# Four column groups for the time-kernel products, eight kernel writes on another queue, and a later second Toeplitz piece

## The chip, the core and the metric

One core of one Trainium2 chip runs the whole program. The metric is the device time of one execution in microseconds (us), and the median over several executions counts.

## What is computed

The input x has 32 rows of 32 channels by 512 steps, that is 1024 tokens of 512 numbers. Two layers follow each other. What matters here, cut from the reference:

```python
# layer 0: a condition matrix per row, then a routed feed-forward net
xt = einsum('bct,bcd->bdt', x, W[condition])          # 1024 tokens of 512
gate = top 2 of 16 experts per token
y  = sum over experts of gate * (silu(xt@w1+b1) * (xt@w2+b2)) @ w3 + b3
z  = silu(xt@sw1+sb1) * (xt@sw2+sb2) @ sw3 + sb3      # shared part
x  = x + y + z
# layer 1: a state space convolution over time, 32 heads, 512 steps
dtA = (-exp(log_A_real) + 1j*A_imag) * exp(log_dt)[:, None]
Cs = C * (exp(dtA) - 1) / A
K  = 2 * einsum('hn,hnl->hl', Cs, exp(dtA * arange(512))).real   # kernel: 32 heads x 512
y  = causal convolution of x (masked by length) with K, plus x * D
x  = x + feed-forward net and layer norm of y
```

The change is about K: how it is computed, written to memory, and read back as a Toeplitz matrix.

## The kernel before

**The expert blocks.** The (token, expert) pairs are sorted into 31 blocks of 128 rows (NB = 31, loop variable n, lines 1512 to 1544 on TensorE). For block n TensorE does 16 matmul instructions for w1 and w2 (L1518), the product with w3 of block n-2 (`block_y`, L1491), and four transposes of the rows of block n+2 (`transpose_x`, L1485). ScalarE makes silu (`bsil`, L771) of block n and copies the transposed rows of block n+2 (`xt`, L759). VectorE makes `bhid` (L1151) and copies block n-2's result into `yout` (L1143), which raises `yout_ok`. GpSimd gathers the token rows of a block from memory (`xg`, L597) and scatters each finished block to `ytok` (L604), seven blocks behind the gathers, by the function `move`.

**The weights.** `ew` is a ring of 14 slots for expert weights (w1 and w2 at 256 KB each by L501, w3 at 256 KB by L503). The queue of SyncE (SP) issues the loads. It runs a loop over n: wait for `yout_ok` n+1, then the loads that `load_step` puts at this n (the loads of blocks 14 to 27 at steps 0 to 18, the last of these at step 18; the loads of blocks 28, 29 and 30 at steps 22, 23 and 24), then possibly a Toeplitz piece.

**The time kernel.** K of a head at time 32 i + j is a product of powers: one factor for i (`lre_k`, `lim_k`: 16 values) and one for j (`rre_k`, `rim_k`: 32 values). One of 16 tiles t holds two heads in its 128 partitions, and its right side has 64 columns, 32 for each head. At block 15 TensorE does 16 tiles times two products (real part L1540, imaginary part L1541), one after the other, with the result in 16 partitions of bank 4 (tiles 0 to 7) and bank 5 (tiles 8 to 15). At block 16 ScalarE copies the two banks into `kout`, 16 partitions by 32 heads by 32 (L786, two copies). After its scatter at `move(15, 22)` GpSimd adds the parameter D in one place of each head (L644), and writes `kout` to `kpad` in memory with two transfers (L645, L646), then goes on with its moves.

**The Toeplitz pieces.** `toeplitz` (L485) reads `kpad` back with overlapping rows: 128 partitions times 6 heads times 512, 1.5 MB a piece, into `toep`. `toep` lies on the same memory as ring slots 0 to 7 of `ew`; piece 0 lies on slots 0 and 1 and the second, third and fourth pieces on the pairs after them. The steps at which the pieces are issued are `TOEP_STEPS = (19, 20, 25, 26)`. Before the first, SP waits for the writes to `kpad` (`kpad_in`). A last piece of 8 heads is read during the convolution.

**Behind the writes.** `sw3h` lies on memory that `kout` uses too. So ScalarE waits at block 21 for `kpad_in` before it writes `sw3h` (L792); behind it stand `bsil` of block 22 and `xt` of block 24.

**Behind the blocks.** TensorE does the `y_product`s of the shared part (L410 to L412), 8 tiles, which VectorE adds into `acc` (`add_y`, L959). SP waits for all scatters (`ys_out`) and loads the pairs of rows of each tile from `ytok` (`yg`, L522, 8 loads of 512 KB, at most four ahead). VectorE adds them with their gates (L1207, two for each tile, `comb_ok`); TensorE transposes each tile (L1572), ScalarE copies it to `u_t` (L800), and the convolution (L1584) begins when all eight are there. In the convolution four heads write to four groups of 32 columns of TensorE, which lie in four groups of 32 partitions of one bank.

Of the kernel before, what the change touches and what calls it, by code (L numbers as in the profile page):

```python
# [38 lines left out]
def adaln_ffn_program(nc, x, cond, length, cond_w, router_w, router_b, router_bias, ew1, eb1, ew2, eb2, ew3, eb3,  # L39
# [45 lines left out]
    TOEP_STEPS = (19, 20, 25, 26)  # L85
# [67 lines left out]
    kout = at(r, "kout", [LI, C, LJ])  # L153
# [137 lines left out]
    drow = at(small, "drow", [1, C])  # L291
# [66 lines left out]
    DIM_HI, RECIP, DECAY, CLAMPED, FOLDED, MASKED, POWERS = range(1, 8)  # L358
# [75 lines left out]
    def _(sp):  # L434
# [19 lines left out]
        sp.wait_ge(b3z_ok, 1)  # L454
# [4 lines left out]
        sp.dma_start(drow[:, :], d_param.rearrange("(o n) -> o n", o=1)).then_inc(l1_in, 16)  # L459
# [45 lines left out]
        for n in range(NB):  # L505
            sp.wait_ge(yout_ok, n + 1)
            for d in range(NB - RING):
                if load_step(d) == n:
                    load(d)
            if n in TOEP_STEPS:  # L510
                g = TOEP_STEPS.index(n)
                if g == 0:
                    sp.wait_ge(kz_in, 16)
                    sp.wait_ge(kpad_in, 32)
                toeplitz(g * TP, g * TP, TP, g)
# [24 lines left out]
    def _(pool):  # L540
# [99 lines left out]
        move(15, 22)  # L640


        pool.wait_ge(kout_ok, 2)
        link(pool.tensor_tensor(kout[0:1, :, LJ - 1], kout[0:1, :, LJ - 1], drow[:, :], ALU.add))  # L644
        pool.dma_start(kpad[:, 0:T - LJ].rearrange("h (i j) -> i h j", j=LJ), kout[1:LI, :, :]).then_inc(kpad_in, 16)  # L645
        pool.dma_start(kpad[:, T - LJ:T].rearrange("h (i j) -> i h j", j=LJ), kout[0:1, :, :]).then_inc(kpad_in, 16)  # L646
        move(22, NB + AHEAD)
# [13 lines left out]
    def _(act):  # L661
# [103 lines left out]
        for n in range(NB):  # L765
# [17 lines left out]
            if n == 16:  # L783
                for j in range(2):
                    act.wait_ge(k_done, j + 1)
                    act.activation(kout[:, j * LI:(j + 1) * LI, :],  # L786
                                   bank[4 + j][0:LI, :].rearrange("p (h j) -> p h j", j=LJ), ACT.Copy, scale=2.0)\
                        .then_inc(kout_ok, 1)
            if n == 21:
                act.wait_ge(kpad_in, 32)  # L790
                act.wait_ge(l1_in, 16 * 7)
                act.activation(sw3h[:, :], sw3raw[:, :], ACT.Copy).then_inc(swh_ok, 1)  # L792
# [77 lines left out]
    def _(dve):  # L870
# [12 lines left out]
        dve.memset(b3p[:, :], 0.0).then_inc(b3z_ok, 1)  # L883
        dve.memset(wbd[:, :, :], 0.0).then_inc(wbd_ok, 1)
# [260 lines left out]
        for n in range(NB):  # L1145
# [35 lines left out]
            elif n == 12:  # L1181
                s4_left_re()
            elif n == 13:
                s4_left_im()
            elif n == 22:
                dve.wait_ge(swh_ok, 3)
                tt(sw3l[:, :], sw3raw[:, :], f(sw3h[:, :]), ALU.subtract).then_inc(swl_ok, 1)
            elif n in (23, 24):
                q = n - 23
                dve.wait_ge(hidh_ok, q + 1)  # L1190
                tt(hidl[:, 2 * q:2 * q + 2, :], hid[:, 2 * q:2 * q + 2, :], f(hidh[:, 2 * q:2 * q + 2, :]), ALU.subtract)\
                    .then_inc(hidl_ok, 1)
# [135 lines left out]
    def _(pe):  # L1328
# [183 lines left out]
        for n in range(NB):  # L1512
# [21 lines left out]
            if n == 15:  # L1534
# [3 lines left out]
                for t in range(HT):  # L1538
                    dst = bank[4 + t // 8][0:LI, t % 8 * 2 * LJ:(t % 8 + 1) * 2 * LJ]
                    pe.matmul(dst, lre_k[:, t, :], rre_k[:, t, :, :].rearrange("p a j -> p (a j)"), start=True, stop=False)  # L1540
                    mm = pe.matmul(dst, lim_k[:, t, :], rim_k[:, t, :, :].rearrange("p a j -> p (a j)"), start=False, stop=True)  # L1541
                    if t % 8 == 7:
                        mm.then_inc(k_done, 1)
# [16 lines left out]
        pe.wait_ge(kout_ok, 2)  # L1560
# [150 lines left out]
```

## Time and profile before

| | |
|---|---|
| median of 3 runs | 356.6 us |
| lowest and highest | 353.71 and 357.53 us |
| the profiled execution | 356.69 us, of which the span of instructions is 354.8 us |
| granted TensorE clock over the span | 0.965 |
| busy: TensorE, VectorE, ScalarE, GpSimd | 326.3, 185.9, 116.6, 102.8 us |

The profile is of one execution. Its times are counted from the start of the span. A line such as L1518 is a line of the program; PE is TensorE, PEld its weight loads, DVE VectorE, ACT ScalarE, POOL GpSimd, and SP the engine that mostly issues transfers. Matmuls are pipelined, so their single durations overlap; the chain of work gives each the time it adds.

### The profile page before, as it was taken

Reading aid. Unit: us, or ns where it says so; the run is one execution under the profiler, and the core shown is the slowest. Engines: PE = TensorE matmul, PEld = TensorE weight load, DVE = VectorE, ACT = ScalarE, POOL = GpSimd, SP = SyncE. Lnnn points to the kernel's source line nnn. Section 1 sums busy time; section 2 is a strip of 40 time slices with the busy share of each in tenths; the row PEclk is TensorE's granted clock in tenths of the full one; section 3 lists DMA queues with packets and bytes.
Section 4 is the critical chain, followed back from the end, with each engine's and each line's share of the span. In section 5 each row is a group of like instructions: output and inputs, shape, how many; then the busy total and the mean of one; then the engine's idle time right before and its main releaser. Section 6 shows DMA issues by size and latency. Waiting matters only on the chain.

```text
span 354.8 us, 5424 instructions
## 1 busy us (share of the span) xinstructions
PE 326.3 (92%) x1915; PEld 243.8 (69%) x1915; DVE 185.9 (52%) x371; ACT 116.6 (33%) x199; POOL 102.8 (29%) x131
## 2 busy tenths in 40 slices
PE   8888999999999899997985799899998999999992
PEld 2456786688887788876673344468887787888871
DVE  4757873879376133641569249536321436433166
ACT  1671220232832143621016633732212424222210
POOL 2230004256577767742400000699200000000000
PEclk9999998999999999998997599999999999999997
DMA  6999901487576769999868991000000000100003
GB/s 201 355 394 399 362 7 30 154 318 223 183 224 229 209 209 316 362 395 399 295 255 276 329 339 47 0 3 0 0 2 0 1 2 30 61 30 0 0 7 113
DMA packets 32312, 59.93 MB, mean 169 GB/s; under 512 B 6680, under 2 KB 7548, under 8 KB 32286
## 3 DMA queue, kind: packets, MB, share of 16 engines
q1 hardware_dynamic: 25182, 48.89, 39.9%
q0 software_dynamic: 5056, 8.49, 7.1%
q10 hardware_dynamic: 2048, 2.21, 1.8%
q8 instruction: 16, 0.26, 0.3%
q14 instruction: 10, 0.08, 0.1%
HBM read 55.02 MB, written 12.40 MB: 190 GB/s over the span
## 4 chain that ended last, share of the span: by engine, by line
PE 75%; DVE 10%; issue 4%; DMA 4%; ACT 4%; POOL 2%; ACTq 0%; DVEq 0%; POOLq 0%
PE bank L1518 13%; PE bank L410 12%; PE bank L411 11%; PE bank L412 11%; PE bank L1491 6%; PE bank L1584 5%; PE bank L1485 3%; DMA xg<-xrow,tokx 2%; DVE acc L1207 1%; PE bank L1332 1%; DMA yg<-ytok 1%; PE bank L1502 1%; PE bank L1382 1%; PE bank L1593 1%; PE bank L1414 1%
## 5 line engine op out<-in xcount | busy, mean ns | idle before, releaser
L1518 PE MATMUL bank<-xt,ew 128*128 128x128 f32 x496 | 61.4, 277 | 2.3 <-issue 2.3
L1518 PEld LDWEIGHTS bank<-xt,ew 128*128 128x128 f32 x496 | 58.5, 193 | 3.6 <-issue 3.4
L597 POOL DMA_INDIRECT xg<-xrow,tokx x31 | 33.0, 1064 | 48.0 <-DVE dstx L1032 29.1
L604 POOL DMA_INDIRECT ytok<-yout,dstx x31 | 32.1, 1034 | 32.3 <-DVE yout L1143 21.7
L1291 DVE TENSOR_TENSOR sq<-rel 128x512 f32<-128x512 f32 x16 | 13.4, 835 | 43.4 <-ACT rel L849 43.4
L1491 PE MATMUL bank<-ew,bhid 128*128 128x512 f32 x62 | 32.5, 610 | 0.0
L759 ACT ACTIVATE xt<-bank 128x512 f32<-128x512 f32 x31 | 18.4, 597 | 33.2 <-PE bank L1485 33.1
L1485 PEld LDWEIGHTS bank<-ident,xg 128*128 128x128 f32 x124 | 15.6, 143 | 17.7 <-issue 13.8
L410 PE MATMUL bank<-dnh,sqh 128*128 128x512 f32 x64 | 25.1, 393 | 1.8 <-DVE sql L1299 1.6
L410 PE MATMUL bank<-ah,uph 128*128 128x512 f32 x64 | 25.1, 392 | 0.0
L411 PE MATMUL bank<-dnl,sqh 128*128 128x512 f32 x64 | 24.9, 390 | 0.0
L411 PE MATMUL bank<-al,uph 128*128 128x512 f32 x64 | 24.9, 389 | 0.0
L412 PE MATMUL bank<-dnh,sql 128*128 128x512 f32 x64 | 24.9, 389 | 0.0
L412 PE MATMUL bank<-ah,upl 128*128 128x512 f32 x64 | 24.9, 389 | 0.0
L651 POOL TENSOR_TENSOR dnl<-dnraw,dnh 128x512 fp32r<-128x512 f32 x8 | 10.5, 1347 | 48.1 <-ACT dnh L816 48.1
L1143 DVE COPY yout<-bank 128x512 f32<-128x512 f32 x31 | 21.4, 690 | 3.9 <-PE bank L1491 1.1
L1151 DVE SCALAR_TENSOR_TENSOR bhid<-bank,b12d,bsil 128x128 f32<-128x128 f32 x15 | 5.3, 351 | 33.7 <-ACT bsil L771 33.7
L1584 PE MATMUL bank<-toep,u_t 128*32 128x512 f32 (+3 forms) x256 | 21.3, 482 | 1.1 <-ACT u_t L800 1.1
L849 ACT ACTIVATE rel<-bank 128x512 f32<-128x512 f32 x16 | 9.6, 599 | 36.8 <-PE bank L412 36.7
L1485 PE MATMUL bank<-ident,xg 128*128 128x128 f32 x124 | 18.8, 276 | 1.7 <-DMA xg<-xrow,tokx 1.7
L1584 PEld LDWEIGHTS bank<-toep,u_t 128*32 128x32 f32 x256 | 8.2, 120 | 13.7 <-issue 11.0
L1299 DVE TENSOR_TENSOR sql<-sq,sqh 128x512 fp32r<-128x512 f32 x16 | 12.0, 750 | 9.8 <-PE bank L412 5.6
(302 smaller groups left out, 600.8 us busy)
## 6 DMA issues: line engine op xcount, KB each, us to landing
ew<-in_L_ffn_ew SPq DMA_DIRECT2D x51, 256.0 KB, 4.1
ew<-in_L_ffn_ew SPq DMA_DIRECT2D x21, 512.0 KB, 9.5
toep<-kpad SPq DMA_DIRECT2D x4, 1536.0 KB, 11.4
yg<-ytok SPq DMA_DIRECT2D x8, 512.0 KB, 4.5
acc<-in_x SPq DMA_DIRECT2D x4, 512.0 KB, 7.2
xrow<-xstage ACTq DMA_DIRECT2D x4, 512.0 KB, 7.0
upraw<-in_L_ffn_up_w SPq DMA_DIRECT2D x1, 2048.0 KB, 10.4
dnraw<-in_L_ffn_down_w SPq DMA_DIRECT2D x1, 2048.0 KB, 13.0
```

The source lines that it names most:

```text
L410: pe.matmul(dst, lh, rh, start=(start and k == 0), stop=False)
L411: pe.matmul(dst, lh, rl, start=False, stop=False)
L412: mm = pe.matmul(dst, ll, rh, start=False, stop=(stop and k == n_k - 1))
L597: pool.indirect_dma_start(xg[:, n % XGS, :], None, xrow, bass.IndirectOffsetOnAxis(ap=tokx[:, n:n + 1].bitcast(U32), axis=0), bounds_check ...
L604: pool.indirect_dma_start(ytok, bass.IndirectOffsetOnAxis(ap=dstx[:, n:n + 1].bitcast(U32), axis=0), yout[:, n % YOS, :], None, bounds_che ...
L759: act.activation(xt[:, n % 2, :, :], bank[n % 2][:, :].rearrange("p (k n) -> p k n", k=KC), ACT.Copy)\
L1143: dve.tensor_copy(yout[:, n % YOS, :], bank[6 + n % 2][:, :]).then_inc(yout_ok, 1)
L1291: tt(sq[:, v % 2, :], rel[:, v % 2, :], rel[:, v % 2, :], ALU.mult).then_inc(sq_ok, 1)
L1485: mm = pe.transpose(bank[n % 2][:, k * P:(k + 1) * P], xg[:, n % XGS, k * P:(k + 1) * P], ident[:, :])
L1491: pe.matmul(bank[6 + n % 2][:, :], bhid[:, n % BHS, :], ew[:, ring(n), W3], start=True, stop=True)\
L1518: mm = pe.matmul(bank[2 + n % 2][:, w * P:(w + 1) * P], ew[:, ring(n), col + k * P:col + (k + 1) * P], xt[:, n % 2, k, :], start=(k == 0), ...
L1584: mm = pe.matmul(bank[g % 3][j * B:(j + 1) * B, 0:T - k * P], u_t[:, h0 + j, k, :], toep[:, (h0 + j) % TS, k * P:T], start=(k == 0), stop= ...
```

## The change

The products are reordered and go to four groups of columns. Tile t = 4 q + m goes to partitions 32 q to 32 q + 15 of bank 4, so all 16 tiles lie in one bank, in four bands of 16 partitions, and the inner loop goes over the four groups. One copy on ScalarE (112 partitions by 256) takes the place of the two. The addition of D (now 112 by 8) moves from GpSimd to VectorE, at block 17. The write to `kpad` moves from GpSimd to SP: two transfers for each of the four bands, eight in all, at step 18 behind the weight loads of that step. GpSimd's moves run through. The Toeplitz pieces are issued at steps 19, 25, 26 and 27.

```diff
-    TOEP_STEPS = (19, 20, 25, 26)
+    TOEP_STEPS = (19, 25, 26, 27)
+    KQ = 4
+    KROWS = 32 * (KQ - 1) + 16
...
-    kout = at(r, "kout", [LI, C, LJ])
+    kout = at(r, "kout", [P, C // KQ, LJ])
...
-        sp.wait_ge(b3z_ok, 1)
+        sp.wait_ge(b3z_ok, 2)
...
-        sp.dma_start(drow[:, :], d_param.rearrange("(o n) -> o n", o=1)).then_inc(l1_in, 16)
+        sp.dma_start(drow[0:P:P // KQ, :], d_param.rearrange("(o n) -> o n", o=KQ)).then_inc(l1_in, 16)
...
+            if n == TOEP_STEPS[0] - 1:
+                sp.wait_ge(s4v_ok, SKIP)
+                for q in range(KQ):
+                    rows = q * P // KQ
+                    heads = kpad[q * C // KQ:(q + 1) * C // KQ, :]
+                    sp.dma_start(heads[:, 0:T - LJ].rearrange("h (i j) -> i h j", j=LJ), kout[rows + 1:rows + LI, :, :])\
+                        .then_inc(kpad_in, 16)
+                    sp.dma_start(heads[:, T - LJ:T].rearrange("h (i j) -> i h j", j=LJ), kout[rows:rows + 1, :, :])\
+                        .then_inc(kpad_in, 16)
             if n in TOEP_STEPS:
                 g = TOEP_STEPS.index(n)
                 if g == 0:
                     sp.wait_ge(kz_in, 16)
-                    sp.wait_ge(kpad_in, 32)
+                    sp.wait_ge(kpad_in, 32 * KQ)
...
-        move(15, 22)
-        pool.wait_ge(kout_ok, 2)
-        link(pool.tensor_tensor(kout[0:1, :, LJ - 1], kout[0:1, :, LJ - 1], drow[:, :], ALU.add))
-        pool.dma_start(kpad[:, 0:T - LJ].rearrange("h (i j) -> i h j", j=LJ), kout[1:LI, :, :]).then_inc(kpad_in, 16)
-        pool.dma_start(kpad[:, T - LJ:T].rearrange("h (i j) -> i h j", j=LJ), kout[0:1, :, :]).then_inc(kpad_in, 16)
-        move(22, NB + AHEAD)
+        move(15, NB + AHEAD)
...
             if n == 16:
-                for j in range(2):
-                    act.wait_ge(k_done, j + 1)
-                    act.activation(kout[:, j * LI:(j + 1) * LI, :],
-                                   bank[4 + j][0:LI, :].rearrange("p (h j) -> p h j", j=LJ), ACT.Copy, scale=2.0)\
-                        .then_inc(kout_ok, 1)
+                act.wait_ge(k_done, 1)
+                act.activation(kout[0:KROWS, :, :], bank[4][0:KROWS, 0:C // KQ * LJ].rearrange("p (h j) -> p h j", j=LJ),
+                               ACT.Copy, scale=2.0).then_inc(kout_ok, 1)
             if n == 21:
-                act.wait_ge(kpad_in, 32)
+                act.wait_ge(kpad_in, 32 * KQ)
...
+        dve.memset(drow[:, :], 0.0).then_inc(b3z_ok, 1)
...
+            elif n == 17:
+                dve.wait_ge(kout_ok, 1)
+                tt(kout[0:KROWS, :, LJ - 1], kout[0:KROWS, :, LJ - 1], drow[0:KROWS, :], ALU.add).then_inc(s4v_ok, 1)
...
-                for t in range(HT):
-                    dst = bank[4 + t // 8][0:LI, t % 8 * 2 * LJ:(t % 8 + 1) * 2 * LJ]
-                    pe.matmul(dst, lre_k[:, t, :], rre_k[:, t, :, :].rearrange("p a j -> p (a j)"), start=True, stop=False)
-                    mm = pe.matmul(dst, lim_k[:, t, :], rim_k[:, t, :, :].rearrange("p a j -> p (a j)"), start=False, stop=True)
-                    if t % 8 == 7:
-                        mm.then_inc(k_done, 1)
+                for m in range(HT // KQ):
+                    for lhs, rhs in ((lre_k, rre_k), (lim_k, rim_k)):
+                        for q in range(KQ):
+                            t = q * HT // KQ + m
+                            mm = pe.matmul(bank[4][q * P // KQ:q * P // KQ + LI, m * 2 * LJ:(m + 1) * 2 * LJ], lhs[:, t, :],
+                                           rhs[:, t, :, :].rearrange("p a j -> p (a j)"), start=(lhs is lre_k),
+                                           stop=(lhs is lim_k))
+                mm.then_inc(k_done, 1)
```

On SP's queue, from the weight loads of step 18 to those of step 22, the order before is this (L501 and L503 load weights, L485 is a Toeplitz piece):

```order
L501 DMA ew<-in_L_ffn_ew 128x512 x2
L503 DMA ew<-in_L_ffn_ew 128x512
L485 DMA toep<-kpad 128x6x512 x2
L497 TENSOR_LOAD eji
L497 ISA x2
L501 ISA
L501 DMA ew<-in_L_ffn_ew 128x512 x2
L503 DMA ew<-in_L_ffn_ew 128x512
```

Two pieces stand ahead of the three last sets of weights. In the changed kernel the same place reads so (L503 and L505 load weights, L517 and L519 write `kout` to `kpad`, L487 is a Toeplitz piece):

```order
L503 DMA ew<-in_L_ffn_ew 128x512 x2
L505 DMA ew<-in_L_ffn_ew 128x512
L517 DMA kpad<-kout 15x8x32
L519 DMA kpad<-kout 8x1x32
L517 DMA kpad<-kout 15x8x32
L519 DMA kpad<-kout 8x1x32
L517 DMA kpad<-kout 15x8x32
L519 DMA kpad<-kout 8x1x32
L517 DMA kpad<-kout 15x8x32
L519 DMA kpad<-kout 8x1x32
L487 DMA toep<-kpad 128x6x512
L499 TENSOR_LOAD eji
```

Eight writes stand between the weights of step 18 and the one piece that is left ahead of the last weights; three pieces follow those weights instead of two.

On TensorE the products at block 15 were one of L1540 and one of L1541 in turn, 16 times:

```order
L1540 MATMUL bank4<-rre_k_71,lre_k_73 16x64
L1541 MATMUL bank4<-rim_k_72,lim_k_74 16x64
L1540 MATMUL bank4<-rre_k_71,lre_k_73 16x64
L1541 MATMUL bank4<-rim_k_72,lim_k_74 16x64
L1540 MATMUL bank4<-rre_k_71,lre_k_73 16x64
```

In the changed kernel they stand in runs of four, one to each group of columns, between the transposes of block 17 and the products of block 16 (L1524):

```order
L1548 MATMUL bank4<-rre_k_71,lre_k_73 16x64 x4
L1548 MATMUL bank4<-rim_k_72,lim_k_74 16x64 x4
L1548 MATMUL bank4<-rre_k_71,lre_k_73 16x64 x4
L1548 MATMUL bank4<-rim_k_72,lim_k_74 16x64 x4
L1548 MATMUL bank4<-rre_k_71,lre_k_73 16x64 x4
L1548 MATMUL bank4<-rim_k_72,lim_k_74 16x64 x4
L1548 MATMUL bank4<-rre_k_71,lre_k_73 16x64 x4
L1548 MATMUL bank4<-rim_k_72,lim_k_74 16x64 x4
L1524 MATMUL bank2<-xt_115,ew_58 128x128 x8
```

Their number is the same (32, each of which the trace shows as two instructions); neighbours now write to different groups.

On ScalarE the copy into `sw3h` and its wait for the writes stay where they are, at block 21; of the changed kernel:

```order
L763 ACTIVATE xt<-bank 128x512 [waits bh_done,bx_done]
L794 ACTIVATE sw3h<-sw3raw 128x1024 [waits l1_in,kpad_in]
L775 ACTIVATE bsil<-bank,b12d 128x128 [waits bhid_ok,bh_done]
L763 ACTIVATE xt<-bank 128x512 [waits bh_done,bx_done]
L797 ACTIVATE hidh<-hid 128x1024
```

The second row is the waiting one, the third is block 22's silu and the fourth block 24's transposed rows; nothing moved in this piece, but what `kpad_in` counts is now eight writes of SP.

## Rows read from the trace of the kernel before

**Rows 1.** the page: the chain by engine, and DMA share in 40 slices

```profile
PE 75%; DVE 10%; issue 4%; DMA 4%; ACT 4%; POOL 2%; ACTq 0%; DVEq 0%; POOLq 0%
...
DMA  6999901487576769999868991000000000100003
```

**Rows 2.** the chain in order of time (start us, us, what), around block 15

```profile
117.92 0.66 PE bank L1485 x4
118.57 0.21 PE bank L1540 x2
...
122.14 0.11 PE bank L1541 x2
122.25 1.98 PE bank L1518 x16
```

**Rows 3.** the chain in order of time, from block 27 to the convolution

```profile
160.10 1.63 issue
161.73 2.63 PE bank L1518 x16
164.35 1.71 PE bank L1491 x2
...
182.82 0.76 DVE acc L1207
```

**Rows 4.** the chain in the convolution: a group of four heads

```profile
206.31 2.29 PE bank L1584 x32
```

**Rows 5.** SP's queue in order of time (start us, us, line, operation)

```profile
140.10 0.38 SPq L503 DMA_DIRECT2D ew<-in_L_ffn_ew  x1
141.27 3.46 SPq L485 DMA_DIRECT2D toep<-kpad  x2
...
151.72 0.86 SPq L501 DMA_DIRECT2D ew<-in_L_ffn_ew  x2
152.67 0.44 SPq L503 DMA_DIRECT2D ew<-in_L_ffn_ew  x1
...
179.35 10.90 SPq L522 DMA_DIRECT2D yg<-ytok  x8
```

**Rows 6.** landing of the second Toeplitz piece (issued at 144.4), by tile

```profile
DMA to landing us min/median/max: 14.2/14.2/14.2
```

**Rows 7.** landing of w1 and w2 of block 28, by line

```profile
DMA to landing us min/median/max: 7.0/7.4/7.7
```

**Rows 8.** landing of w3 of block 28 (issued at 152.7), by line

```profile
DMA to landing us min/median/max: 9.0/9.0/9.0
```

**Rows 9.** landing of the fourth Toeplitz piece (issued at 166.8), by tile

```profile
DMA to landing us min/median/max: 8.5/8.5/8.5
```

**Rows 10.** busy time in stretches: engines, granted clock, DMA share, GB/s

```profile
150.00:160.00 10.00, 9.46 (x68) 7.63 (x66) 4.76 (x8) 3.40 (x7) 5.01 (x5) 1.00 1.05 396
160.00:170.00 10.00, 8.27 (x48) 6.69 (x49) 1.99 (x4) 1.42 (x4) 1.97 (x2) 0.83 1.05 395
170.00:180.00 10.00, 9.98 (x45) 7.14 (x44) 5.10 (x9) 0.37 (x1) 3.93 (x4) 1.00 0.56 208
```

**Rows 11.** ScalarE in order of time, blocks 21 to 24

```profile
141.48 1.05 ACT L792 ACTIVATE sw3h<-sw3raw 128x1024 fp32r<-128x1024 f32 x1
...
144.07 0.60 ACT L759 ACTIVATE xt<-bank 128x512 f32<-128x512 f32 x1 [0.93 <-PE bank L1485]
```

**Rows 12.** TensorE in order of time: block 24's products

```profile
146.96 1.95 PE L1518 MATMUL bank<-xt,ew 128*128 128x128 f32 x16
```

**Rows 13.** transfers by line: KB each, median us from issue to landing

```profile
out<-acc SPq DMA_DIRECT2D x8, 256.0 KB, 2.0
leni<-in_itok_B SPq DMA_DIRECT2D x4, 0.1 KB, 5.7
```

**Rows 14.** landing of the scatter issued at 160.5, by line

```profile
DMA to landing us min/median/max: 6.6/6.6/6.6
```

**Rows 15.** landing of the first two loads of yg, by line

```profile
DMA to landing us min/median/max: 3.2/3.7/4.1
```

More of the change, by code:

```diff
@@ L290, in adaln_ffn_program @@
     halfpi = at(small, "halfpi", [P, 1])
-    drow = at(small, "drow", [1, C])
+    drow = at(small, "drow", [P, C // KQ])
     top8 = at(small, "top8", [P, NT, 8])
@@ L357, in adaln_ffn_program @@
     SINE, COSINE, EXPS = 1, 2, 3
-    DIM_HI, RECIP, DECAY, CLAMPED, FOLDED, MASKED, POWERS = range(1, 8)
+    DIM_HI, RECIP, DECAY, CLAMPED, FOLDED, MASKED, POWERS, SKIP = range(1, 9)
     lgt_done, lgt_ok = (sem(s) for s in ("lgt_done", "lgt_ok"))
@@ L1559, in _ @@
         pe.wait_ge(l1_in, 16 * 7)
-        pe.wait_ge(kout_ok, 2)
+        pe.wait_ge(kout_ok, 1)
         pe.wait_ge(swl_ok, 3)
```

## The prediction, made before the changed kernel was run

> **What bounds the kernel now.** I read the page first. TensorE carries 75% of the chain that ended last, and the transfer engines are at nine or ten tenths in the slices from about 130 to 175 us [rows 1]. So this is a kernel bound by TensorE with a stretch in its middle where transfers are full too. Then the chain in order of time, where the change sits. The reader is to see two places. Around block 15 the time-kernel products run from 118.57 to 122.25, 3.7 us in which nothing else stands on the chain [rows 2]. Before block 28 TensorE stands still: the products start at 161.73 behind 1.6 us of "issue", and that is a wait for weights, since SP issued block 28's w3 at 152.67 and it landed 9.0 us later, at 161.7 [rows 3, 5, 8]. The granted clock tells the rest of that price. In the stretch from 160 to 170 it is 0.83 in the mean, so the engine spent about a third of it at the lower of its two levels (1.2 instead of 2.4 GHz), and block 26's w3 product took 1.71 us there [rows 3, 10]; in the undisturbed blocks the same pair takes half of that. That costs some 1.7 us beside the pause. Why were the weights late? SP's queue, the third view, shows two Toeplitz pieces issued from 141.27, ahead of the weights of 151.72 [rows 5]. The second, issued at 144.4, landed 14.2 us later, at 158.6 [rows 6]; block 28's w1, issued at 151.7, landed 7.0 us later, at 158.7 [rows 7]. So SP's transfers land one behind the other, and what stands ahead in the queue is paid by what stands behind.
>
> **The products (L1540, L1541).** Before, 64 instructions of 64 columns take 3.7 us, 57 ns each, in the chain [rows 2]. The convolution already uses four groups of columns: one group of heads there is 32 instructions of 512, 384, 256 and 128 columns (8 each, 10,240 columns) in 2.29 us, 4,470 columns a us [rows 4], against 64 x 64 / 3.7 = 1,110 here. So four groups do run side by side, four times as fast. The bounds are 0.9 us (all of the factor) and 3.7 us (none). I take 1.5 us, since these instructions are short: a saving of 2.2 us at block 15, between 0 and 2.8. The gathers behind them are ahead of TensorE from there on (GpSimd no longer stops for the writes), so the 2.2 us arrive at block 24 if nothing else is late.
>
> The Trainium skill (TensorEngine Tiling (Array Packing), Performance Considerations) states an overhead of about 60 cycles for each matmul, and warns not to tile a dimension that is already small. By it 64 instructions cost 64 x 25 ns = 1.6 us at the least, and the saving would be 2.1 us; the trace has no four-group run with so few columns. The sum below does not change by it.
>
> **Copy, addition, other small edits.** One copy of 256 columns replaces two of 512 on ScalarE; VectorE gets one addition of 8 columns at block 17 and one small memset at the start; both engines wait for TensorE there, so both are worth nothing. GpSimd loses one addition and two transfers, which hid in its lead.
>
> **The eight writes.** They stand on SP behind the weights of step 18. Before, the w3 of that step was issued at 140.10 and took 0.38 us [rows 5]. 2.2 us earlier that is 138.3. Small transfers take SP 0.42 us each (the four of `leni` went out one after the other), so the last is issued at about 141.7. Before, the writes went out from GpSimd near 129 and nobody waited for them. From both sides: the unhindered `out` takes 2.0 us to land, the small `leni` behind large loads 5.7 us [rows 13]. So the last lands between 143.7 and 147.4. The w3 ahead should be in by 142.5, so I am nearer to the first: 144.5. Two things wait for it.
>
> First ScalarE, at block 21. It wrote `sw3h` at 141.48, that is 139.3 when 2.2 us earlier, and now starts at 144.5. Behind it come 1.05 us of its own, the silu of block 22 and the copy `xt` of block 24, which was at 144.07 to 144.67; TensorE needed that copy at 146.96 [rows 11, 12]. It had 2.3 us of slack. Now the copy ends at 144.5 + 1.95 = 146.5, and TensorE would like it at 144.8: a new stall of 1.7 us at block 24 (0.9 to 4.6 by the bounds). It may bring the clock down for a while, as the pause before block 28 did, 1.7 us more. So of the 2.2 us won at block 15 about 0.5 are left at block 24, or none.
>
> Second, Toeplitz piece 0 goes out at about 144.9, not 141.27.
>
> **The second piece moved.** With one piece ahead instead of two, and SP's queue at about 1.5 MB in 7.5 us (two pieces from 141.3 to 158.6 with a set of weights), piece 0 is in by 153 and block 28's w3 by about 157. TensorE wants it at 159. The 2.3 us pause and the 1.7 us of low clock go. So TensorE's blocks end 2.2 - 1.7 + 4.0 = 4.5 us earlier (2.8 if the new stall lowers the clock).
>
> **What is late next.** The expert blocks are not the end of this stretch. The first addition of a `yg` pair was at 182.82 [rows 3]: VectorE had finished the sixth shared tile then, and `yg` had been issued at 179.35 and landed 3.2 us later, at 182.55 [rows 5, 15]. Two things ended nearly together, and the change moves only one of them freely. `yg` stands in SP's queue behind all Toeplitz pieces. Before, the queue's work from piece 0 (141.27) to the last piece (166.8 + 8.5 = 175.3) was 34.0 us long [rows 5, 9], and then the queue was idle: the share is 1.05 from 150 to 170 and 0.56 from 170 to 180 [rows 10]. The same four pieces and three sets of weights now start at 144.9, with three pieces at the end instead of two. They cannot be quicker than the full transfer engines; I take 32.3 us, less than 34.0 because the first three us before were not full. So the last piece is in at 177.2. The last scatter, issued near 172, needs some 5 to 6 us under such load (6.6 at 160.5 [rows 14]) and is in at 177.3. Then `yg` goes out at 177.5 and lands at 180.7. TensorE's side would allow 178.3. The additions start at about 180.7 instead of 182.82: 2.1 us gained, and behind it additions, transposes and convolution go as before.
>
> **Sum.** 356.69 - 2.1 = 354.6 us for the profiled execution; that execution is within 0.1 us of the median of the runs, 356.6, so I forecast 354.6. In other words: TensorE's side gains 2.8 to 4.5 us, and about half is lost since the idle time of the transfer engines at 175 to 180 was the room it would need.
>
> **Rivals.** One per cent, about what a measurement of this kernel can tell from no change, is 3.6 us.
>
> A. The forecast, 354.6. For it speaks the full share up to 175 us; against it that the 32.3 us are an estimate.
>
> B. TensorE's side decides. If the writes land at 143.7 and the queue is quicker, ScalarE's stall is 0.9 and the additions follow TensorE: -2.2 + 0.9 - 4.0 = -5.3, so 351.4. For it: the unhindered landing of 2.0. Against it: `yg` would have to land at 177.5.
>
> C. The four groups do not overlap on such short products. Then the block-15 saving is 0, step 18 comes 2.2 us later, the writes land at 146.7, the last piece at 179.4, and `yg` at 182.9: 356.7. Against it: rows 4.
>
> D. Slower: the writes land late. At 7.5 us behind their issue (149.2) ScalarE stalls TensorE by 6.4 us, TensorE's side gains nothing (2.2 - 6.4 - 1.7 + 4.0 = -1.9), piece 0 goes at 149.6, the last piece is in at 181.9 and `yg` at 185: 358.8. It decides from a landing at about 146.6 on; each us behind that costs one. For it: 512 runs of 128 B each, on a queue that stays busy, and the 5.7 of `leni`. Against it: the queue ahead of them is nearly empty.
>
> The Trainium skill (DMA: Bandwidth & Descriptors, Anatomy of one DMA) puts most of a transfer's fixed 2 us in the receipt of the write, heaviest when it goes to HBM, and its Specifications want 512 B for line rate. By that page D would be likelier; the trace's `out`, a write of 2 KB runs, shows 2.0 us, and no row shows runs of 128 B landing.
>
> E. The queue's work is not compressed at all: three pieces in a row with the last scatters take 34.5 us, `yg` lands at 182.9: 356.8. For it: the scatters took 6.6 us in the full stretch.
>
> **Chances.** A 0.42, B 0.2, C 0.1, D 0.14, E 0.14. Faster by over 1%: B and the near edge of A, 0.27. Slower by over 1%: the far part of D, 0.09. The rest, 0.64, is within 1%. The range goes from B's 351.4 to D's 358.6.
>
> **What would show it.** Right: the products near 1.5 us; eight issues from about 138 to 142; ScalarE's `sw3h` starting at 144 to 145 with an idle time before it that a transfer ended; block 24's products 1 to 2 us late; no pause before block 28 and no low clock there; a DMA share of one up to 176 or 177; `yg` issued at 177 to 178. Wrong: products still at 3.7 us (C); `sw3h` after 146 (D); `yg` issued before 176, or additions that start right behind VectorE's sixth shared tile (B).

## The result and the profile after

| | before | changed |
|---|---|---|
| median of 12 runs beside each other | 356.98 us | 359.7 us |
| lowest and highest | 353.71 and 360.27 us | 356.63 and 361.37 us |
| ratio, 95% interval | | 1.010, 1.0070 to 1.0129 |
| the profiled execution | 356.69 us | 357.48 us, span 355.5 us |

The changed kernel is 1.0% slower. The forecast was 354.6 us (351.4 to 358.6), so sign and size are wrong. A second set of 12 runs of the same kernel, with other kernels beside it, gave 358.38 us against 356.66 (ratio 1.006, 1.0025 to 1.0095), which is slower too, though just inside the stated range; its profiled execution took 360.5 us. I read both profiles. The ratios here and below leave out the runs that took over 1.5% longer than the fastest of their kernel and the medians don't, so the two can differ, most of all for kernel 8, where 7 of 12 runs are left out (at most 2 for the other changed kernels, 6 of 35 for the kernel before).

The profiled execution of the changed kernel is 2.2 us below its median, and it was ahead before the change could act: block 0's products began at 66.3 us there and at 67.8 before. The profiled executions of all kernels differ in this way. Their time-kernel products at block 15, where the change first acts on TensorE, begin anywhere from 116.56 to 120.48 us. So a time read from one profile can't be set against a time from another as it stands, and where I compare two profiles I count from the start of these products: 118.57 before, 116.56 in the changed kernel, 119.87 in its repeat.

The chain of the changed kernel in order of time (start us, us, what), from block 15 to the first addition of a `yg` pair:

```profile
116.56 1.02 PE bank L1548 x64
...
140.81 3.61 DMA kpad<-kout
...
145.75 0.50 ACT xt L763
...
146.29 3.78 PE bank L1524 x16
150.07 1.71 PE bank L1497 x2
151.78 0.81 PE bank L1491 x4
...
174.28 5.91 DMA ytok<-yout,dstx
...
180.42 3.23 DMA yg<-ytok
...
183.67 0.77 DVE acc L1213
```

Against [rows 2] the products take 1.02 us instead of 3.7. Against [rows 3] there is no wait before block 28 any more. But a transfer that was on no chain before, the last write of `kout`, now stands on it, and behind it block 24's products take 3.78 us instead of 1.79, its w3 product 1.71 instead of 0.86. At the end the additions begin at 183.67, behind a scatter of 5.91 us and `yg`. Counted from the products that is 67.1 us, where it was 64.3 before (182.82).

SP's queue of the changed kernel (start us, us, line, operation), the counterpart of [rows 5]:

```profile
136.18 0.41 SPq L505 DMA_DIRECT2D ew<-in_L_ffn_ew  x1
136.64 0.49 SPq L517 DMA_DIRECT2D kpad<-kout  x1
...
140.81 0.63 SPq L519 DMA_DIRECT2D kpad<-kout  x1
144.49 0.40 SPq L487 DMA_DIRECT2D toep<-kpad  x1
153.77 0.86 SPq L503 DMA_DIRECT2D ew<-in_L_ffn_ew  x2
...
162.15 6.53 SPq L487 DMA_DIRECT2D toep<-kpad  x3
180.42 10.69 SPq L533 DMA_DIRECT2D yg<-ytok  x8
```

The eight writes go out from 136.64 to 141.4, 0.6 us each; the Toeplitz piece waits for them until 144.49; block 28's weights go out at 153.77, 2 us later than before [rows 5], though the rest of the kernel was ahead. The late pieces (those behind block 30's weights, three now and two before) go out from 162.15, 45.6 us behind the products. Before it was 41.2 us:

```profile
159.78 7.42 SPq L485 DMA_DIRECT2D toep<-kpad  x2
```

ScalarE around the wait, the counterpart of [rows 11]; the bracket is its idle time and what ended it:

```profile
136.31 0.60 ACT L763 ACTIVATE xt<-bank 128x512 f32<-128x512 f32 x1 [0.93 <-PE bank L1491]
144.44 1.06 ACT L794 ACTIVATE sw3h<-sw3raw 128x1024 fp32r<-128x1024 f32 x1 [7.53 <-DMA kpad<-kout]
145.65 0.59 ACT L763 ACTIVATE xt<-bank 128x512 f32<-128x512 f32 x1
```

ScalarE stood still for 7.53 us, from 136.9 on, for the writes. The copy `xt` of block 24 (145.65) is behind it, and TensorE waited for that copy for 3.84 us:

```profile
146.29 3.78 PE L1524 MATMUL bank<-xt,ew 128*128 128x128 f32 x16 [3.84 <-ACT xt L763]
```

The stretches, counterpart of [rows 10] (busy time and count of TensorE, its weight loads, VectorE, ScalarE and GpSimd; then granted clock, DMA share, GB/s):

```profile
140.00:150.00 10.00, 6.16 (x34) 5.39 (x33) 4.07 (x6) 4.43 (x7) 2.16 (x2) 0.78 0.68 242
150.00:160.00 10.00, 10.00 (x64) 7.81 (x63) 4.26 (x7) 2.89 (x6) 6.00 (x7) 0.88 0.71 223
160.00:170.00 10.00, 10.00 (x69) 8.04 (x69) 3.34 (x7) 2.66 (x6) 3.73 (x4) 1.00 1.02 359
170.00:180.00 10.00, 9.98 (x41) 7.26 (x39) 5.67 (x9) 0.00 (x0) 2.99 (x4) 1.00 1.00 383
```

Two things are new: a clock of 0.78 and 0.88 in the two stretches from 140, and a DMA share of 0.68 and 0.71 where it was 1.05 from 150 to 160 [rows 10]. The transfer engines have a hole, and the stretch from 170 to 180, half idle before, is full.

The repeat, whose products began 3.3 us later, shows the same:

```profile
147.36 1.06 ACT L794 ACTIVATE sw3h<-sw3raw 128x1024 fp32r<-128x1024 f32 x1 [7.14 <-DMA kpad<-kout]
```

```profile
144.34 2.99 DMA kpad<-kout
...
149.21 3.78 PE bank L1524 x16
...
177.14 6.34 DMA ytok<-yout,dstx
...
183.69 3.23 DMA yg<-ytok
```

### The profile page after: what moved, and what is told of

Read it like the earlier page. It is cut to its first block, busy times and chain, and to the rows that moved or that the text cites. A ratio compares the mean times of both kernels' runs of the same rounds, so it can differ in the third digit from the quotient of the medians.

```text
span 355.5 us, 5430 instructions
## 1 busy us (share of the span) xinstructions
PE 323.6 (91%) x1915; PEld 241.8 (68%) x1915; DVE 185.8 (52%) x373; ACT 115.5 (32%) x198; POOL 101.1 (28%) x128
## 4 chain that ended last, share of the span: by engine, by line
PE 66%; DVE 10%; DMA 9%; issue 5%; ACT 4%; POOL 2%; SPq 2%; ACTq 1%; DVEq 0%; POOLq 0%
PE bank L1524 12%; PE bank L412 11%; PE bank L413 10%; PE bank L414 10%; PE bank L1497 5%; PE bank L1592 5%; PE bank L1491 3%; DMA yg<-ytok 3%; DMA xg<-xrow,tokx 2%; DMA rb<-in_L_ffn_router_bias 2%; DMA ytok<-yout,dstx 2%; DVE acc L1213 1%; PE bank L1508 1%; PE bank L1388 1%; PE bank L1601 1%
## 5 line engine op out<-in xcount | busy, mean ns | idle before, releaser
L1524 PE MATMUL bank<-xt,ew 128*128 128x128 f32 x496 | 62.6, 281 | 3.8 <-ACT xt L763 3.8
L1524 PEld LDWEIGHTS bank<-xt,ew 128*128 128x128 f32 x496 | 59.7, 197 | 5.2 <-ACT xt L763 4.1
L1592 PE MATMUL bank<-toep,u_t 128*32 128x512 f32 (+3 forms) x256 | 20.3, 463 | 1.1 <-ACT u_t L802 1.1
```

The costliest lines, as they stand in the source:

```text
L1524: mm = pe.matmul(bank[2 + n % 2][:, w * P:(w + 1) * P], ew[:, ring(n), col + k * P:col + (k + 1) * P], xt[:, n % 2, k, :], start=(k == 0), ...
L1592: mm = pe.matmul(bank[g % 3][j * B:(j + 1) * B, 0:T - k * P], u_t[:, h0 + j, k, :], toep[:, (h0 + j) % TS, k * P:T], start=(k == 0), stop= ...
```

## The experiments

I held two theories at first. **W**: ScalarE's wait for the eight writes is what costs. **Q**: three Toeplitz pieces in a row, ahead of `yg` in SP's queue, are what costs. Each kernel below was timed in five rounds beside the kernel before; the medians of before were 356.76 us beside kernels 1 to 4, 356.66 beside the repeat and kernels 5 to 7, 355.72 beside 8 and 9, and 355.38 beside 10. Each kernel had 12 runs, kernel 6 only 6.

| kernel | median us | ratio to before, 95% interval |
|---|---|---|
| changed, again | 358.38 | 1.0060 (1.0025 to 1.0095) |
| 1 no wait of ScalarE | 355.04 | 0.9965 (0.9932 to 0.9998) |
| 2 before, late second piece | 356.34 | 1.0003 (0.9967 to 1.0039) |
| 3 writes at step 17 | 354.57 | 0.9944 (0.9904 to 0.9984) |
| 4 changed, old steps | 356.67 | 0.9991 (0.9950 to 1.0033) |
| 5 writes at 17, no wait | 353.59 | 0.9942 (0.9903 to 0.9982) |
| 6 one group at a time | 361.35 | 1.0144 (1.0094 to 1.0194) |
| 7 as 5, fourth piece behind `yg` | 352.00 | 0.9878 (0.9837 to 0.9919) |
| 8 as 5, old steps | 355.98 | 0.9941 (0.9890 to 0.9991) |
| 9 before, late pieces, fourth behind `yg` | 355.52 | 1.0014 (0.9983 to 1.0044) |
| 10 as 7, last piece ahead of `down_w` | 351.17 | 0.9868 (0.9837 to 0.9899) |

The profiles give three more numbers for each, all counted from the start of the products at block 15 (us, one execution each):

| kernel | products begin | first late piece goes out | `yg` goes out | the span ends |
|---|---|---|---|---|
| before | 118.57 | 41.2 | 60.8 | 236.2 |
| changed | 116.56 | 45.6 | 63.9 | 238.9 |
| changed, again | 119.87 | 45.1 | 63.8 | 238.6 |
| 1 | 119.68 | 38.6 | 58.2 | 233.9 |
| 2 | 120.33 | 41.2 | 59.7 | 234.8 |
| 3 | 119.65 | 38.6 | 57.1 | 233.3 |
| 4 | 118.46 | 43.1 | 60.5 | 236.7 |
| 5 | 118.59 | 38.5 | 57.1 | 233.3 |
| 6 | 118.66 | 44.9 | 63.4 | 237.9 |
| 7 | 118.41 | 38.6 | 54.6 | 230.8 |
| 8 | 119.52 | 38.6 | 59.6 | 234.5 |
| 9 | 118.86 | 41.2 | 57.8 | 234.5 |
| 10 | 120.48 | 38.6 | 54.6 | 230.7 |

The column of the late pieces shows how TensorE sets SP's queue: the late pieces wait for a step of the loop, that is for `yout_ok`. Where TensorE has no stall up to there, the first goes out at 41.2 us with the old products and at 38.5 to 38.6 with the new ones, earlier by 2.6 to 2.7 us, the whole saving (3.68 - 1.02). Only the kernels in which ScalarE waits long (changed, its repeat, 4 and 6) are later.

**Changed, again.** No edit.

> The changed kernel once more, beside the others. Both theories: 2 to 4 us above the kernel before, ScalarE idle for more than 5 us ahead of sw3h, low clock behind block 24.

It held in the traces. In time it is 1.7 us over before by the medians and 2.1 by the ratio, so it lies at the edge of the 2 us named. The two sets give 1.0060 and 1.0100, with intervals that overlap.

**1. No wait of ScalarE.** The section on the kernel before says that `sw3h` lies on memory of `kout`. That was my error: `sw3h`, `sw3l`, `hidh` and `hidl` take the first 24,576 bytes of each partition of that region and `kout` starts at 25,984. What `hidh` and `hidl` do overwrite is the sides of the products, and ScalarE has waited for the products at block 16. So the wait can go.

```diff
             if n == 21:
-                act.wait_ge(kpad_in, 32 * KQ)
                 act.wait_ge(l1_in, 16 * 7)
```

> The changed kernel without ScalarE's wait for the writes at block 21 (kout lies behind sw3h, sw3l, hidh and hidl in memory, so nothing needs it). Theory W (the wait of ScalarE on the eight writes is what costs: 7.5 us idle on ScalarE, block 24's products 4 us late, then 3.2 us of low clock): block 24 starts without a stall, no low clock near 145 to 152, yg is issued about 3 us earlier since the weights behind it and the last pieces go out earlier, and the time is 3 us or more below the changed kernel, at or below the kernel before (354 to 357 when before is 357). Theory Q (three Toeplitz pieces at the end of the queue, ahead of yg, are what costs): the blocks end earlier but yg does not, and the time stays within 1 us of the changed kernel (about 360).

355.04 us, 3.3 below the repeat of the changed kernel. ScalarE and SP, and the chain:

```profile
139.94 1.05 ACT L793 ACTIVATE sw3h<-sw3raw 128x1024 fp32r<-128x1024 f32 x1
```

```profile
147.46 0.40 SPq L487 DMA_DIRECT2D toep<-kpad  x1
...
158.26 7.73 SPq L487 DMA_DIRECT2D toep<-kpad  x3
177.89 10.71 SPq L533 DMA_DIRECT2D yg<-ytok  x8
```

`sw3h` starts at 139.94 with no idle time, although the piece still goes out at 147.46 behind the writes. Block 28's weights go out at 150.20 instead of 156.70 in the repeat, and `yg` at 177.89 instead of 183.69. Theory W holds. Q's forecast, within 1 us of the changed kernel, fails. This kernel also says what the late writes cost SP's queue: piece 0 goes out as late as in the repeat (27.8 and 27.5 us behind the products), and `yg` still goes out 5.6 us earlier. With early writes as well (kernel 5) it goes out another 1.1 us earlier. So nearly all of the cost came through ScalarE's wait.

**2. The kernel before with the late second piece alone.**

```diff
-    TOEP_STEPS = (19, 20, 25, 26)
+    TOEP_STEPS = (19, 25, 26, 27)
```

> The kernel before with only the steps of the Toeplitz pieces changed from 19, 20, 25, 26 to 19, 25, 26, 27. Theory W: the pause ahead of block 28 (2.3 us and 1.7 us of low clock) goes, yg moves by half of that: 1.5 to 3 us below the kernel before. Theory Q: the pause goes too, but the pieces pile up ahead of yg and the time is 1 to 2 us above the kernel before.

Ratio 1.0003. W wanted 1.5 to 3 us less and missed. Q wanted 1 to 2 us more, and the interval (to 1.4 us more) can't rule out its near edge. The chain:

```profile
161.21 1.79 PE bank L1518 x16
...
173.66 6.19 DMA ytok<-yout,dstx
...
180.07 3.19 DMA yg<-ytok
```

The pause is gone: block 28's products run at 161.21 for 1.79 us, at full clock. `yg` goes out at 180.07, but the products began 1.76 us later than before; counted from them it is 1.0 us earlier (59.7 against 60.8). The pause and its low clock had cost TensorE some 4 us, and the last scatter goes out 4.2 us earlier (53.3 against 57.5). But among the three pieces it takes 6.19 us to land, where before `yg` went out 3.3 us behind its issue at 176.09. So removing the pause alone brings `yg` forward by a quarter of its price, and the time can't tell that from nothing: the end of this stretch is set by the last scatter and by SP's queue.

**3. The writes one step earlier.**

```diff
-            if n == TOEP_STEPS[0] - 1:
+            if n == TOEP_STEPS[0] - 2:
                 sp.wait_ge(s4v_ok, SKIP)
```

> The changed kernel with the eight writes one step earlier (step 17, where SP has no weights to load). Theory W: the last write lands about 3 us earlier than 144.4, ScalarE's idle time falls from 7.5 to about 4.5 us, block 24 is about 1 us late instead of 4, and the time is 3 to 5 us below the changed kernel. Theory Q: within 1 us of the changed kernel.

354.57 us, 3.8 below the repeat of the changed kernel. ScalarE and SP:

```profile
141.51 1.06 ACT L794 ACTIVATE sw3h<-sw3raw 128x1024 fp32r<-128x1024 f32 x1 [1.50 <-DMA kpad<-kout]
```

```profile
141.56 0.39 SPq L487 DMA_DIRECT2D toep<-kpad  x1
149.74 0.82 SPq L503 DMA_DIRECT2D ew<-in_L_ffn_ew  x2
...
176.73 10.73 SPq L533 DMA_DIRECT2D yg<-ytok  x8
```

The writes are in at 141.5, 5.8 us ahead of the repeat's 147.33 (5.6 counted from the products) and not 3, since the weights of step 18 (whose issues took from 137.81 to 140.1 in the repeat) no longer stand ahead of them. So the idle time is 1.50 us, less than the 4.5 forecast, and block 24 isn't late at all. W holds again, from the other side: the wait stays in the program and costs nothing once the writes are early enough.

**4. The changed kernel with the old steps.**

```diff
-    TOEP_STEPS = (19, 25, 26, 27)
+    TOEP_STEPS = (19, 20, 25, 26)
```

> The changed kernel with the old steps of the pieces (19, 20, 25, 26). Theory W: the stall at block 24 stays at 4 us with its low clock, and the pause ahead of block 28 comes back in part, since the second piece stands ahead of its weights: the time is 0 to 3 us above the changed kernel. Theory Q: the second piece fills the hole in the transfers at 143 to 156, yg goes out earlier, and the time is 2 us or more below the changed kernel.

356.67 us, 1.7 below the repeat: W said 0 to 3 above, Q 2 or more below, so both missed. ScalarE's wait, TensorE's, and SP's queue:

```profile
146.20 1.06 ACT L794 ACTIVATE sw3h<-sw3raw 128x1024 fp32r<-128x1024 f32 x1 [7.37 <-DMA kpad<-kout]
```

```profile
148.05 2.05 PE L1524 MATMUL bank<-xt,ew 128*128 128x128 f32 x16 [3.69 <-ACT xt L763]
```

```profile
146.25 2.65 SPq L487 DMA_DIRECT2D toep<-kpad  x2
...
178.98 10.67 SPq L533 DMA_DIRECT2D yg<-ytok  x8
```

ScalarE waits for 7.37 us as in the changed kernel, and `yg` goes out at 178.98 against 183.69 (60.5 against 63.8 counted from the products). A second piece now fills the hole: the DMA share from 150 to 160 is 1.04 instead of 0.73, and the last scatter takes 3.31 us. But the trace shows a second difference of the same size. TensorE stalls for 3.69 us here too, and its clock stays at the higher level behind it: block 24's products take 2.05 us, where the repeat lost 3.1 us to the low clock. So how much of the 3.3 us the steps brought, as Q has it, and how much the clock, is open. The intervals of this kernel (to 1.0033) and of the repeat (from 1.0025) touch, so even the gain in time is likely, not proven.

From here on the theory was **M**: ScalarE's wait delays TensorE and, through `yout_ok`, the last weights and pieces, so the transfers have a hole; the end is then set by the last scatter and by SP's queue.

**5. Writes at step 17 and no wait.** The edits of 1 and 3 together.

> Writes at step 17 and no wait of ScalarE for them. Theory M (ScalarE's wait delays TensorE and, through it, the last weights, so that the transfers have a hole; the end is then set by the last scatter and by SP's queue): with the writes at step 17 the wait was 1.5 us long, inside ScalarE's slack of 2.3 us, so this is within 0.5 us of the kernel with the writes at step 17 alone, about 354 to 355. Rival R (each wait for the writes costs in full): 1 to 1.5 us below that kernel.

353.59 us, ratio 0.9942 against 0.9944. The times alone can't decide: the intervals are 1.4 us wide on each side, and the medians differ by 1.0 us, the near edge of R. The traces can: counted from the products `yg` goes out at 57.09 here and at 57.08 in kernel 3, and the span ends at 233.3 in both. M holds and R falls; a wait of 1.5 us inside ScalarE's slack costs nothing.

**6. One group at a time.** The same products in the same places, with the groups in the outer loop:

```diff
-                for m in range(HT // KQ):
-                    for lhs, rhs in ((lre_k, rre_k), (lim_k, rim_k)):
-                        for q in range(KQ):
+                for q in range(KQ):
+                    for m in range(HT // KQ):
+                        for lhs, rhs in ((lre_k, rre_k), (lim_k, rim_k)):
```

> The changed kernel, but the products go through one group of columns after the other (q as the outer loop), so neighbours share a group: the same results in the same places. Theory M: the products take 3.6 us again instead of 1.0; what follows (step 18, the writes, ScalarE's wait) comes 2.6 us later as a whole, so the time is 2 to 3 us above the changed kernel. Rival E (the saving at block 15 is eaten by ScalarE's wait): within 0.7 us of the changed kernel.

```profile
118.66 3.06 PE bank L1548 x64
...
182.10 3.32 DMA yg<-ytok
```

```profile
148.97 3.02 PE L1524 MATMUL bank<-xt,ew 128*128 128x128 f32 x16 [2.38 <-ACT xt L763]
```

The products take 3.06 us instead of 1.02, so the saving of the four groups comes from running side by side. Whether it reaches the end of this kernel is open, for the times and the trace disagree. The kernel is 361.35 us, 3.0 above the repeat (ratios 1.0144 and 1.0060, whose intervals just touch), from 6 runs, and against the first set (1.0100, up to 1.0129) the intervals overlap more. In the trace TensorE's stall is 2.38 us instead of 3.46, the low clock behind it costs 1.9 us instead of 3.1, and `yg` goes out 63.4 us behind the start of the products, not later than the 63.8 of the repeat. That is rival E: the wait eats the saving. What shows that the saving can arrive is the pair of kernels 2 and 3, with the same steps and no stall: the late pieces go out 2.65 us earlier in 3, `yg` 2.7, the span ends 1.5 earlier, and the ratio is 0.9944 against 1.0003.

**7. The fourth piece behind `yg`.** As 5, and:

```diff
-    TOEP_STEPS = (19, 25, 26, 27)
+    TOEP_STEPS = (19, 25, 26)
...
+        toeplitz(3 * TP, 3 * TP, TP, 3)
         sp.dma_start(upraw[:, :, :], up_w.rearrange("(k p) m -> p k m", p=P)).then_inc(up_in, 16)
```

> Writes at step 17, no wait of ScalarE, and the fourth Toeplitz piece issued behind all loads of yg (ahead of up_w) instead of at step 27; it is needed only by the fifth group of heads. Theory M: the last scatter is alone sooner, lands in 2 to 4 us instead of 6.2, yg is issued at about 174 instead of 177, and the time is 2 to 3 us below the kernel with the writes at step 17. Rival V (VectorE's additions set the end, yg is no bound): within 0.7 us of it.

```profile
169.10 3.65 DMA ytok<-yout,dstx
...
172.97 3.27 DMA yg<-ytok
...
199.54 12.46 DMA toep<-kpad
```

The last scatter takes 3.65 us, not 6.2; `yg` goes out at 172.97, and the kernel takes 352.0 us (ratio 0.9878). M holds, and the rival that VectorE sets the end falls: VectorE's first addition starts when `yg` has landed. `yg` moved by 2.5 us counted from the products (57.1 in kernel 5), and so did the end of the span; the medians give 1.6 us. The last piece of the convolution is on the chain now. The 12.46 us are its way from issue to landing, not a wait. TensorE had other groups of heads to do and stood still for 0.44 us:

```profile
212.05 2.36 PE L1592 MATMUL bank<-toep,u_t 128*32 128x512 f32 x32 [0.44 <-DMA toep<-kpad]
```

**8. As 5 with the old steps.** The edit of 4.

> Writes at step 17, no wait of ScalarE, and the old steps of the pieces (19, 20, 25, 26). Theory M (the last scatter and SP's queue set the end): the pause ahead of block 28 comes back on TensorE (2 to 3 us and low clock), but the queue's work begins as early as before, so yg moves by 1.5 us at most: within 1.5 us of the kernel with steps 19, 25, 26, 27 (353.6). Rival P (TensorE's pause costs what it shows): 3 to 5 us above that kernel, 357 to 358.

```profile
158.42 2.98 issue
161.40 3.51 PE bank L1523 x16
```

The pause is back in full (2.98 us ahead of block 28, then 3.51 us for its products), and TensorE loses more than 4 us. What the kernel loses is open. The ratio is 0.9941, that of kernel 5 (0.9942), but it rests on 5 of 12 runs. The median of all 12 is 2.4 us above that of kernel 5. The profiled execution (356.15 us, near that median) has `yg` 2.5 us later than kernel 5 and the end of the span 1.2 us later. M allowed 1.5 us for the time and for `yg`, and P wanted 3 to 5. So less than the pause arrives, but neither M's numbers nor P's are confirmed.

**9. The kernel before with the queue of 7.** The edit of 7 in the kernel before.

> The kernel before (one group of products, writes from GpSimd) with pieces at steps 19, 25, 26 and the fourth behind all loads of yg. Theory M: the pause goes, the last scatter lands sooner, yg is issued about 2.5 us earlier than with the late piece alone (180.1 there): 353 to 355, and the 2.6 us of the products are what separates it from the kernel of four groups with the same queue (352.0). Rival N (the products' saving is nothing in the end): within 0.7 us of 352.0.

355.52 us, ratio 1.0014. M wanted 353 to 355 and missed a little; N (no loss against 352.0) falls clearly.

```profile
172.19 4.24 DMA ytok<-yout,dstx
176.66 3.33 DMA yg<-ytok
...
203.69 12.57 DMA toep<-kpad
```

`yg` goes out at 176.66, 1.9 us earlier than in kernel 2 counted from the products (57.8 against 59.7). The last piece takes 12.57 us to land, and TensorE stands still for 0.58 us before it. The span ends only 0.2 us earlier than in kernel 2; most of what was won at `yg` isn't seen at the end, and I haven't shown where it went. Kernel 7 has the same queue, sends `yg` 3.2 us earlier and is 1.4% faster: the four groups, with early writes, are what it has more.

**10. The last piece ahead of `down_w`.** As 7, and:

```diff
-        sp.dma_start(dnraw[:, :, :], down_w.rearrange("(j p) n -> p j n", p=P)).then_inc(dn_in, 16)
         sp.wait_ge(conv_done, (C - TS) // 4)
         toeplitz(0, TS, C - TS, TS // TP)
+        sp.dma_start(dnraw[:, :, :], down_w.rearrange("(j p) n -> p j n", p=P)).then_inc(dn_in, 16)
```

> The kernel with writes at step 17, no wait of ScalarE and the fourth piece behind yg (352.0), with down_w loaded behind the last Toeplitz piece instead of ahead of it. There the last piece was issued at 199.5 with up_w and down_w ahead of it in the queue, and the convolution waited for it until 212.05. Theory M (SP's transfers land in the order of issue): the last piece lands in 10 us or less, the convolution's seventh group starts 1 to 3 us earlier, down_w lands near 215, in time for its copies: 1 to 2 us faster, 350 to 351. Rival D (down_w is then late for ScalarE's copies, which stand ahead of the last copy of the convolution): 1 us slower or more.

Transfers by line in the stretch from 184 us on (KB each, us to landing):

```profile
toep<-kpad SPq DMA_DIRECT2D x1, 2048.0 KB, 9.2
dnraw<-in_L_ffn_down_w SPq DMA_DIRECT2D x1, 2048.0 KB, 15.0
```

The last piece lands in 9.2 us instead of 12.5 and the convolution no longer waits. 351.17 us, ratio 0.9868 against 0.9878 for kernel 7: the interval tells it from the kernel before, not from kernel 7. The wait that went was 0.44 us long, so M's 1 to 2 us were not there to be won. Rival D, 1 us slower or more, didn't come.

## Why the prediction was wrong

**The step that failed: what ScalarE's wait costs, and where.** The forecast gave the new stall of TensorE one price, 1.7 us, and let none of it reach `yg`: it took SP's queue from piece 0 to the last piece as 32.3 us of work that starts when the writes have landed. The runs show another path. The stall was 3.84 us in the profile and 3.46 in the repeat, and the low clock behind it, which I had left as "may be" and at 1.7 us, took 3.2 us more (3.78 - 1.79, 1.71 - 0.86, 0.81 - 0.44) and 3.1. These 7.0 and 6.6 us are more than the 2.7 won at block 15 and the 4.0 of the pause ahead of block 28. And they pass to SP's queue in full, for the late pieces wait for TensorE's blocks: the first goes out 45.6 and 45.1 us behind the products, where the kernels without the stall have 38.6. `yg` follows: 63.9 and 63.8 instead of the 58.9 of the forecast (177.5 less 118.57). Kernel 1 takes the wait away and nothing else, with the writes as late as in the changed kernel, and `yg` goes out at 58.2. Kernel 3 leaves the wait and makes the writes early, and it goes out at 57.1. The queue's work that I took as 32.3 us lasted 37.1 and 36.9 (144.49 to 181.6 and 147.41 to 184.3), and in kernel 1, with piece 0 as late, 30.9. The DMA shares of 0.68 and 0.71 are the sign of this: with one piece ahead and the next loads held back, the queue ran dry, and its work was done at the end, where `yg` stands.

**The eight writes.** I put the last landing 6.2 us behind the end of the issue of the w3 ahead of them (138.3 to 144.5). It was 7.8 us (136.59 to 144.42) and in the repeat 7.2 (140.11 to 147.33). The issues are what I had too short: the eight took SP 4.85 us instead of 3.4, 0.6 us each instead of 0.42, for I took `leni`'s transfers, with one number to a row, as the nearest row. The landing was right: 3.0 us behind the end of the last issue, and 2.4 in the repeat, against 2.8. In the forecast's own times, with products at 118.57, the writes were in at 146.4 and 146.0. That explains the length of the stall (3.84 instead of 1.7) but not the result, since by the forecast's sum only a landing behind 146.6 makes the kernel slower.

The Trainium skill (DMA: Bandwidth & Descriptors, Anatomy of one DMA) describes its fixed 2 us for transfers that GpSimd issues, and these went out on SP. From the start of the last issue to the landing it was 3.6 and 3.0 us, 1 to 1.6 over the 2.0 of `out`; that goes the way the page's rule would have it, but no run here separates the length of the runs from the load on the queue.

**Rival D** (358.8) came closest to the measured 359.7 and 358.4, with a chance of 0.14. It had the place right, late writes that ScalarE waits for. Its number is luck. Its condition, a landing at 149.2, was not met, and it charged the loss to piece 0 going out late, which cost 1.1 us (kernel 1 against kernel 5), and not to TensorE holding back the late pieces. Its sum is also off by itself: with 3.5 us from the last piece to the landing of `yg`, as in A and C, it gives 359.3. The upper end of the range, 358.6, is neither of these numbers.

**The products: right, and low.** I forecast 1.5 us (0.9 to 3.7); they took 1.02. The rule of the Trainium skill (TensorEngine Tiling (Array Packing), Performance Considerations), about 60 cycles of overhead for each matmul, would have given 1.6 us by my estimate; here 64 instructions of 64 columns took 1.02, 16 ns each. The trace doesn't agree with it for neighbours in different groups. Kernels 2 and 3 show that the saving can reach `yg` whole; in the changed kernel the stall ate it.

**The late second piece.** I was right that the pause goes, and right that the gain would be cut off at `yg`. Kernel 2 gives the size: 1.0 us of 4.0 arrive at `yg`, and the ratio can't tell that from nothing. The cause is the last scatter, which takes 6.19 us among three late pieces, and 3.31 and 3.17 in kernels 4 and 8 with two.

**The forecast's structure** (additions begin when `yg` lands, behind the last scatter) held in every profile but that of the kernel before. With the writes at step 17 the changed kernel has the time that I had forecast, 354.57 us against 354.6. The agreement is partly luck: `yg` goes out at 57.1 there, 1.8 us earlier than the forecast's 58.9.

## What to carry to other kernels

When work moves to another queue, look for every wait on its completion, not only for the one that the edit is about, and ask of each whether the memory map still needs it; one that was always past may come to decide. Small transfers in a row on one queue cost their issue times in a chain: put them into a step of the queue that has nothing else to send. Price a stall with what it holds back on other queues, not only with its own length. And a pause on the busiest engine is worth its length only if what follows it isn't waiting for a full queue: take the pause away alone, in one line, before building on it. When two profiles are compared, find first how far apart they were before the change could act.

## What the runs showed of the hardware

Neighbouring matmuls in four groups of 32 columns took 16 ns each at 64 columns, and one group at a time 48 ns (1.02 and 3.06 us for 64). The latter is itself less than the 57 ns of the kernel before, which kept to one group throughout; no run here says why.

A write of 15 x 8 runs of 128 bytes took SP 0.46 to 0.49 us to issue in the changed kernel, and one of 8 runs from a single partition 0.63 to 0.71: the smaller one takes longer. A pair costs SP as much as a set of expert weights (1.2 us).

A stall of TensorE of about the same length was followed by the lower clock level (1.2 GHz) in one execution and not in another. Behind 3.84 us in the changed kernel, and 3.46 in its repeat, the clock was low for some 7 us (the mean was 0.50 from 146 to 152 in the changed kernel). Behind 3.63 us in kernel 8 it was low for some 3.5 us, and behind the 2.38 us of kernel 6 too (0.50 from 150 to 152 and 0.69 to 154). Behind 3.69 us in kernel 4 it stayed at 1.00. So the length of the stall doesn't settle it, and no run here says what does.

The last scatter took 5.9 to 6.3 us with three Toeplitz pieces issued ahead of it (changed, its repeat, kernels 1, 2, 3, 5 and 6), and 3.2 to 4.2 us with two (4, 7, 8, 9 and 10).
